# Two-layer sequence kernel on one NeuronCore: the last state product in two other PSUM banks, and the opening of the recurrence in another order

## The reference, cut to what matters

```python
xn = _layernorm(x, axis=-1)
x = x + _L0_attn_ref(xn, ...) + _L0_ffn_ref(xn, ...)
xn = _layernorm(x, axis=-1)
x = x + _L1_attn_ref(xn, ...) + _L1_ffn_ref(xn, ...)
```

```python
def step(carry, inp):
    W, bb = carry
    Z1 = xk_c @ W + bb
    x_hat = (Z1 - mu) / std
    gxh = (g * x_hat + be - (xv_c - xk_c)) * g
    grad_x = (HD * gxh - gxh.sum(-1) - x_hat * (gxh * x_hat).sum(-1)) / (HD * std)
    dW = einsum('bhkc,bhkd->bhcd', eta * xk_c, grad_x)
    Wn, bn = W - dW, bb - (eta * grad_x).sum(-2)
    Zq = xq_c @ Wn + bn
    out = xq_c + g * ((Zq - mu2) / std2) + be
```

## Time and profile before

| | |
|---|---|
| median of 3 runs | 926.8 us (926.56 to 928.77) |
| profiled execution | 926.01 us, of which the profile's span is 924.2 us |
| PE busy | 861.4 us, 93% of the span |
| DVE busy | 776.4 us, 84% |
| POOL busy | 638.0 us, 69% |
| ACT busy | 553.7 us, 60% |
| mean granted clock of PE | 0.985 of full |

### The profile page before, as it was taken

One profiled execution on the slowest core, in us unless ns is written; L12 is line 12 of the kernel. 1 busy time (PEld: TensorE's weight loads), 2 busy tenths in 40 slices (PEclk: granted clock), 3 DMA queues, 4 the chain that ended last, 5 costly groups with the idle time before them and its releaser, 6 DMA issues.

```text
span 924.2 us, 19886 instructions
## 1 busy us (share of the span) xinstructions
PE 861.4 (93%) x7832; PEld 602.6 (65%) x7832; DVE 776.4 (84%) x1180; ACT 553.7 (60%) x845; POOL 638.0 (69%) x582
## 2 busy tenths in 40 slices
PE   2778999999997899999999999999999999999997
PEld 2566878788776797565576575565565665665564
DVE  7889999999997647978878979878979878879876
ACT  4546566766653555576576566576566666566663
POOL 5387788888883144786785876775876875776873
PEclk9799999999997999999999999999999999999999
DMA  8100000000000601010121120120120110120110
GB/s 216 50 2 2 2 2 3 2 2 4 3 2 1 182 2 41 40 67 22 46 67 33 49 79 21 46 66 24 59 78 22 46 67 23 60 78 21 46 53 24
DMA packets 25077, 38.29 MB, mean 41 GB/s; under 512 B 9444, under 2 KB 15608, under 8 KB 22936
## 3 DMA queue, kind: packets, MB, share of 16 engines
q1 hardware_dynamic: 23352, 34.74, 12.1%
q10 hardware_dynamic: 1632, 2.27, 0.8%
HBM read 28.29 MB, written 1.43 MB: 32 GB/s over the span
## 4 chain that ended last, share of the span: by engine, by line
PE 54%; DVE 24%; issue 12%; POOL 7%; ACT 3%; DMA 1%; SPq 0%; POOLq 0%; DVEq 0%
PE bank L1240 11%; PE bank L1242 10%; PE bank L1241 10%; DVE hdh L1034 6%; PE bank L1550 3%; PE quad L1582 3%; DVE add L1043 3%; PE bank L1406 2%; DVE mx L1027 2%; POOL arena L1151 2%; PE quad L1295 2%; POOL arena L1157 2%; PE bank L1601 1%; PE bank L1395 1%; PE quad L1378 1%
## 5 line engine op out<-in xcount | busy, mean ns | idle before, releaser
L1027 DVE TENSOR_REDUCE mx<-quad 128x4 f32<-128x2048 f32 x64 | 146.4, 2287 | 37.5 <-PE quad L1582 37.4
L1208 POOL CAST hdh<-xn 128x512 fp32r<-128x512 f32 x96 | 66.1, 689 | 155.1 <-ACT xn L662 155.1
L679 ACT ACTIVATE ex<-quad 128x2048 f32<-128x2048 f32 x64 | 120.6, 1884 | 59.0 <-PE quad L1592 59.0
L1210 POOL TENSOR_TENSOR hdl<-hd,hdh 128x512 fp32r<-128x512 f32 x96 | 129.6, 1350 | 7.7
L1210 POOL TENSOR_TENSOR hdl<-xn,hdh 128x512 fp32r<-128x512 f32 x96 | 128.9, 1343 | 7.7
L1240 PE MATMUL bank<-hdh,W2h 128*128 128x512 f32 x256 | 113.8, 445 | 6.1 <-DVE hdl L1037 5.4
L662 ACT ACTIVATE xn<-bank,b1c 128x512 f32<-128x512 f32 x128 | 87.8, 686 | 26.8 <-POOL hdl L1210 19.2
L662 ACT ACTIVATE hd<-bank,b1c 128x512 f32<-128x512 f32 x112 | 76.9, 687 | 44.7 <-PE bank L1242 29.1
L1241 PE MATMUL bank<-hdh,W2l 128*128 128x512 f32 x256 | 101.1, 395 | 0.0
L1242 PE MATMUL bank<-hdl,W2h 128*128 128x512 f32 x256 | 101.1, 395 | 0.0
L1240 PE MATMUL bank<-cH,W1h 128*128 128x512 f32 x192 | 81.0, 422 | 0.7 <-DVE cL L1054 0.7
(11 more groups left out here) (315 smaller groups left out, 2167.4 us busy)
## 6 DMA issues: line engine op xcount, KB each, us to landing
cwB<-gate_rows SPq DMA_DIRECT2D x16, 1024.0 KB, 4.7
kx<-kqh SPq DMA_DIRECT2D x32, 64.0 KB, 2.1
qx<-kqh SPq DMA_DIRECT2D x32, 64.0 KB, 2.1
W1r<-in_L_ffn_W SPq DMA_DIRECT2D x1, 1024.0 KB, 10.0
kx<-kql SPq DMA_DIRECT2D x16, 64.0 KB, 2.1
qx<-kql SPq DMA_DIRECT2D x16, 64.0 KB, 2.1
rec<-rec_rows SPq DMA_DIRECT2D x32, 32.0 KB, 2.2
out<-fin SPq DMA_DIRECT2D x4, 256.0 KB, 2.3
```

The lines of the kernel that those rows point to most:

```text
L679: act.activation(ex[:, t % 2, :, :], quad[:, :, :], ACT.Exp, scale=float(AD) ** -0.5).then_inc(ROUND["exps_ready"], 1)
L1027: dve.tensor_reduce(mx[:, t, :, 0], quad[:, :, :], AX_X, ALU.max, negate=True).then_inc(ROUND["score_max"], 1)
L1208: pool.tensor_copy(hdh[:, m % RING, :], tile(n)).then_inc(ROUND["pool_split"], 1)
L1210: pool.tensor_tensor(hdl[:, m % RING, :], tile(n), hdh[:, m % RING, :], ALU.subtract).then_inc(ROUND["pool_split"], 1)
```

## The change

The last four banks become one tensor, `rest`, so that two of them can be addressed together. The last Zq, block 35 in s, is put into banks 4 and 5 instead of 2 and 3. It gets bias rows of its own, which wait for the U and the queries of those banks and not for `normed`. Its squares go to the buffer `sqz`. The gather of batch 0 moves from in front of `bias_rows(34)` and `att(34)` to one place behind `state_q(35)`. All four `turn_weights` of batch 0 move in front of the last output product `att(35)`, into banks 1, 4, 5 and 0.

In the opening, ACT squares block 0's Z and takes its root before the sigmoid; DVE splits its four operations of 1024 columns into two sets of four of 512 (`targets(0)` in front of the root, `targets(1)` behind `xhat(0)`); POOL does `wql` before `scaled(0)`; two of the router's four logit matmuls move behind `state(0)`; the output weights' products move to steps 1 and 3 of PE, the latter in front of the bias; the exponential of the router moves from ACT's step 1 to its step 4, and a part of `wog` from step 4 to step 3.

```diff
-        bank = [quad[:, n, :] for n in range(4)] + [ctx.enter_context(nc.psum_tensor(f"bank{n}", [P, 512], F32)) for n in range(4, 8)]
+        rest = ctx.enter_context(nc.psum_tensor("rest", [P, 4, 512], F32))
+        bank = [quad[:, n, :] for n in range(4)] + [rest[:, n, :] for n in range(4)]
...
+        zq_last = rest[:, 0:2, 0:256].rearrange("p h (a c) -> p a h c", a=4)
+        LAST_Q = 4 * NC + 3
...
-        EARLY = (4, 5, 0, 1, 4)
+        EARLY = (0, 1, 4, 5, 0)
...
             for s in range(4 * NC + 6):
                 if s == 0:
-                    squares(0), take_xk(0)
+                    squares(0), take_xk(0), deviation(0), take_u(0), rates()
...
                 if s == 4 * NC + 5:
-                    take_weights(0, 0), take_weights(0, 1)
+                    take_weights(0, 0), take_weights(0, 1), take_weights(0, 2), take_weights(0, 3)
                 take_queries(s), deviation_q(s), take_att(s - 2), take_keys(s)
...
-                if s == 1:
-                    act.wait_ge(choice_step, 2)
-                    act.activation(rkp[:, 1, :], lgt[:, :], ACT.Exp, bias=es[:, 0:1], accum_out=es[:, 1:2]).then_inc(choice_exp, 1)
-                    act.activation(warm[:, :], C("ln_eps"), ACT.Sqrt)
-                if s in (4, 5):
+                if s == 4:
+                    choice()
+                if s in (3, 5):
...
+            def targets(n):
+                w = slice(512 * n, 512 * n + 512)
+                dve.scalar_tensor_tensor(out=wul[:, w], in0=wu[:, w], scalar=1.0 / HD, in1=wuh[:, w], op0=ALU.mult, op1=ALU.subtract).then_inc(wu_low, 1)
+                link(dve.scalar_tensor_tensor(out=gb2[:, 0, w], in0=gb2[:, 0, w], scalar=1.0 / HD, in1=gb2[:, 1, w], op0=ALU.mult, op1=ALU.mult))
+                link(dve.tensor_copy(gbr[:, w], gb2[:, 0, w]))
+                dve.tensor_tensor(gbr[32:33, w], gb2[32:33, 0, w], gbr[32:33, w], ALU.subtract).then_inc(target_ready, 1)
+
+            targets(0)
...
             for s in range(4 * NC + 1):
-                scaled(s)
                 if s == 0:
                     pool.wait_ge(kq_high, 2)
                     pool.tensor_tensor(wql[:, :], wq[:, :], wqh[:, :], ALU.subtract).then_inc(wq_low, 1)
+                scaled(s)
...
-                    if s > 4:
+                    if s == LAST_Q:
+                        pe.wait_ge(CHUNK["u_taken"], 4 * NC)
+                        pe.wait_ge(CHUNK["queries_taken"], 4 * NC)
+                    elif s > 4:
                         pe.wait_ge(CHUNK["normed_ready"], s - 4)
...
-                if s == 4 * NC + 2:
-                    pe.wait_ge(CHUNK["keys_taken"], 4 * NC)
-                    pe.wait_ge(CHUNK["gx_ready"], 4 * NC)
-                    gather(0, range(2))
-                elif s == 4 * NC + 4:
-                    gather(0, range(2, NT))
-                XK_(s), bias_rows(s), state_q(s), state(s), target(s)
+                XK_(s), bias_rows(s), state_q(s), state(s)
+                if s == 4 * NC + 3:
+                    pe.wait_ge(CHUNK["state_updated"], 4 * NC)
+                    gather(0, range(NT))
+                if s == 0:
+                    logits(2)
+                    logits(3).then_inc(choice_logits, 1)
+                target(s)
+                if s == 3:
+                    pe.wait_ge(wq_turned_taken, 2)
+                    for a in range(NP):
+                        last = pe.matmul(misc[:, 0:P], wqT[:, a, :], wo[:, a, :], start=(a == 0), stop=(a == NP - 1), skip_group_check=True)
+                    last.then_inc(out_weights, 1)
...
-                if s == 4 * NC + 5:
-                    pe.wait_ge(CHUNK["state_updated"], 4 * NC)
-                    turn_weights(0, 1)
                 att(s - 2), keys(s), dW(s - 2)
-                if s == 4 * NC + 5:
-                    turn_weights(0, 2), turn_weights(0, 3)
+                turn(s - 1)
                 if s == 4 * NC + 4:
-                    pe.wait_ge(CHUNK["queries_taken"], 4 * NC)
-                    turn_weights(0, 0)
-                turn(s - 1)
+                    for g in range(E0 // 4):
+                        turn_weights(0, g)
```

80 lines of the change are left out of this document (42 added, 38 removed).

## The result

The changed kernel takes **918.31 us** (median of 4 runs, 917.75 to 920.55), the kernel before 927.05 beside it (4 runs). The ratio is 0.9907, 95% interval 0.9885 to 0.9929: faster, by 0.7 to 1.15%. The forecast was 919.6 in 916.0 to 923.0. In the profiled executions the span went from 924.2 to 916.0, 8.2 less; the sum of the terms had been 7.2.

The account below looks back on a forecast made before the run. The prediction saw a closed ring in the steady recurrence and chains of waits in the opening and end. Terms +0.2, -3.1, +0.3 and -4.6 sum to -7.2, from 926.8 to 919.6 us, range 916.0 to 923.0.

Parts of the forecast that it names:

- Block 0: Opening: `xhat` ends earlier, but stalls and target work spend it; last sum at 43.6 instead of 43.39, +0.2 us.
- The stall of 2.8: Opening, block 0: a DVE target operation beside POOL's `wql` is held until about 2.8 us.
- the second one: Opening, block 0: behind `xhat`, DVE's second target set stalls against POOL's `scaled(0)`, 1.2 us.
- Block 4: Opening: moving two output-weight products off PE's path removes DVE's 3.10 idle; -3.1 us, between 0 and -3.1.
- The exponential: ACT's step 4, ahead of block 5's squares: 3.6 us against 3.3 idle a block; +0.3, between 0 and +3.6.
- The end: End of the recurrence: DVE's waits shrink and batch 1's gather comes earlier; -4.6 us, between -0.5 and -5.5.
- the new wait ahead of `weighted(2)`: End: DVE waits for batch 1's gather and turnings until 304.8, against a start of 310.34 before.
- the 0.9 that was taken: End: allowance for the last products at the lower clock, 3.2 us instead of 2.3, giving -4.6.
- the full 5.5: End: gain at `weighted(2)` with the last product at full clock, 304.8 instead of 310.34.
- What lies behind: From 320 on nothing changes; expert weights land near 315 for matmuls from 324.37 and stay hidden; 0 us.
- a sign of error: End: a DVE wait for the expert weights was listed among signs that would show the forecast wrong.
- The main risk of the forecast: End: a rival had the lower clock last through `att(34)`, `turn(35)` and the turnings; 922.3 us, chance 0.10.

Follow-up runs that it names:

- Experiment 5: Changed kernel with POOL's `wql` moved behind `gx_xhat(0)`: 917.09 us, ratio 0.9881 to the kernel before.
- experiment 3: Changed kernel with the two output-weight products put back behind `dW(1)` in PE's step 3: 922.88 us, ratio 0.9953 to the kernel before.
- Experiment 7: Changed kernel with ACT copying `turn(34)` ahead of block 35's root and product `att(35)` behind batch 1's turnings: 916.29 us, ratio 0.9872 to the kernel before.
- 9: Changed kernel with block 35's Zq put back into banks 2 and 3: 920.81 us, ratio 0.9941 to the kernel before.
- 10: Changed kernel with turnings 2 and 3 of batch 0's weights put back behind `att(35)`: 919.76 us, ratio 0.9926 to the kernel before.
- 1: Kernel before with only the changed opening, keeping its old end: 923.15 us, ratio 0.9959 to the kernel before.
- 6: Changed kernel with ACT copying `turn(34)` ahead of the root of block 35's Zq: 915.89 us, ratio 0.9871 to the kernel before.
- 11: Changed kernel with 11 and 4 identity transposes where PE idles ahead of the last eight matmuls: 917.36 us, ratio 0.9899 to the kernel before.
- 12: Changed kernel with `wql` behind `gx_xhat(0)`, `turn(34)` copied ahead of the root, and transposes before the last matmuls: 912.91 us, ratio 0.9853 to the kernel before.
- 2: Kernel before with only the changed end (banks, gather, turnings), keeping its old opening: 922.58 us, ratio 0.9948 to the kernel before.
- 4: Changed kernel with block 0's old order (sigmoid ahead of squares, target work undivided): 920.20 us, ratio 0.9922 to the kernel before.
- 8: Changed kernel with `wql` behind `gx_xhat(0)`, `turn(34)` copied first and `att(35)` behind batch 1's turnings: 914.97 us, ratio 0.9863 to the kernel before.

## Why the prediction was right

Point by point, by its own terms:

- **Block 0: +0.2 forecast, -0.2 measured.** The stall of 2.8 was right in size (2.82 for 0.68) and the second one too (1.76). With the old order put back, block 0 ends at 43.30: worth nothing, as said. Experiment 5 shows that the stall held it: move POOL's instruction away, and 1.84 arrive at block 4.
- **Block 4: -3.1 forecast, -3.16 measured, nearly half by another cause.** The prediction laid all of DVE's idle 3.10 to the two products. They carry 1.73. The other 1.4 goes with PE's lower clock from 60 to the start of the first product in before (against the same rows of experiment 3: 2.96 instead of 2.18 from the start of the bias, L1362, to `dW(1)`, 1.06 instead of 0.63 from there to the product, 2.14 instead of 1.88 to the next one, 1.47 in all), a stretch that in the changed opening falls elsewhere. The rows stood at hand: the product took 2.30 in the earlier trace rows and its like 1.95 to 2.05 elsewhere, and it was read as its price. The step "DVE idles 3.10 us, because PE makes two products for the output weights first" was wrong by 1.4, and the size came out right by luck.
- **The exponential: +0.3 forecast, 0.1 at most measured**, from the shift of block 5 against that of block 4. No run puts it back alone.
- **The end: -4.6 forecast, -5.05 measured.** The chain came in the order given, the new wait ahead of `weighted(2)` included. With block 33's shift of 3.0 added to the times measured, so that they compare with the forecast, `att(34)` was expected at 292.5 (292.34), the fourth turning's end at 297.7 (298.86), the gather at 300.6 (301.32), `weighted(2)` at 304.8 (305.31). The lower clock cost more than the 0.9 that was taken: besides `att(34)` with its last pair (2.95 from start to end, forecast 2.3 at full clock) it slowed `turn(35)` (1.08) and the first turnings (0.83), and the fourth turning ended 1.16 later than the full-clock working had it. Behind it two steps were shorter than priced, from there to the gather 2.46 instead of 2.9 and from the gather to `weighted(2)` 3.99 instead of 4.2. That leaves 0.5 off the full 5.5.
- **What lies behind: 0 forecast, 0 measured** between the two profiles. DVE does wait 1.02 for W1, which had been named as a sign of error; the wait is off the path, as PE's expert matmuls (L1521) start at 312.66 without it, 2.85 behind the start of the last turnings (2.87 before). The working had this reserve wrong. It took 8.8 to landing from the row of a 0.5 KB transfer and looked at PE's need at 324.37. W1 itself has 1024 KB, was issued at 307.68 in before and landed 10.0 later, at 317.68, just ahead of DVE's cast:

```profile
W1r<-in_L_ffn_W SPq DMA_DIRECT2D x1, 1024.0 KB, 10.0
317.73 1.22 DVE L941 CAST W1h<-W1r 128x2048 fp32r<-128x2048 f32 x1
```

  There was nothing to spare on DVE (the cast starts 0.05 behind the landing), and 0.66 between the end of the cast and PE in the kernel after. Experiment 7 shows what happens when it is used up.
- **The median** fell by 8.7 and the profiled execution by 8.2, to 917.81. The forecast had carried over before's 0.8 between the two; 0.5 stood there after.

The main risk of the forecast lay where it was put, in the clock at the end, and its size is now known: the changed end takes 29.26 at full clock and 30.6 at 0.89. The 33.22 with the bank back, at 0.79, holds a wait besides.

## What to carry to other kernels

When PE's rows on a path are longer than the same form elsewhere, look at the granted clock of that stretch before you price an instruction: behind a moved wait the slow stretch can fall elsewhere, and the gain or loss is then laid to the edit. Between DVE and POOL, ask for each long POOL instruction what DVE issues beside it, and put the one that nobody needs yet where DVE waits. A product that releases transfers has a due time on both sides; read when what it releases lands before moving it.

## What the runs showed of the hardware

- **The lock between DVE and POOL** goes instruction by instruction, and the first to start keeps it. `wul` took 2.82 beside `wql` and 0.69 without. Cutting DVE's work in half didn't help, since `wql` had started 0.08 before it. It holds the other way too: POOL's `scaled(0)`, started 0.16 behind DVE's second `wul`, took 1.65, and 1.26 in before. The Trainium skill (SBUF — State Buffer, "Who interferes with whom") says that the first to start holds the shared ports for its whole instruction; the trace agrees, with 2.82 for 0.69.
- **The lower clock comes in stretches whose place changes between executions of the same instructions.** In the opening, which is the same in the kernels after, 9, 10 and 1, the granted clock is 0.72 from 54 to 60 in after, and 1.00 there but 0.72 to 0.78 from 72 to 78 in the other three; from 54 to 60 PE is 5.5 to 5.8 of 6 us busy in all four. In 7, with the same opening again, it is 1.00 from 54 to 78. What decides it stays open.
- **The last eight matmuls** (0.22 us from one pair to the next at full clock, 0.43 at the lower) are such a place: full clock in the profiles of before, after, 1, 6, 9, 11 and 12, the lower for half or more of them in 2, 3, 4, 5, 7, 8 and 10, for 0.8 to 1.7 us. Four runs each of the two kernels with transposes there (11 and 12) lie within 1.04 and 0.56 us of each other, four of the change within 2.8, but four of 9, without transposes, within 1.05. Whether the transposes hold the clock is not shown, for want of the same kernel seen in both ways.
